# Down products of a mixture of experts in high and low parts: three fp32r products in place of one f32 product

## The reference

```python
shared = silu(flat @ sg) * (flat @ su) @ sd
probs = softmax(flat @ router_w)
topk_p, topk_i = top_k(probs, 2)
...
h = silu(einsum('nd,edf->nef', flat, wg)) * einsum('nd,edf->nef', flat, wu)
eo = einsum('nef,efd->ned', h, wd)
routed = einsum('ned,ne->nd', eo, cw)
return shared + routed
```

## Time and profile before

| What | Value |
|---|---|
| Median of 3 runs | 1467.71 us (1465.85 to 1470.97) |
| Profiled execution, own time | 1471.52 us |
| Its span | 1469.8 us (1.7 us of the time lie around it) |
| TensorE busy | 1393.9 us, 95% of the span |
| VectorE, ScalarE, GpSimd busy | 854.6, 795.2, 844.4 us |
| Mean granted clock of TensorE | 0.98 |
| The 15 expert blocks, first gate product to last down product | 1303 to 1462 us |

### The profile page before, as it was taken

How to read it: one execution, slowest core, us unless ns; L and a number is a source line. 1 busy time by engine, 2 the same in 40 slices (tenths; PEclk the granted TensorE clock), 3 DMA queues, 4 the chain that set the end, 5 groups by cost and what they waited for, 6 DMA issues and landing times. The chain is left out here.

```text
span 1469.8 us, 25247 instructions
## 1 busy us (share of the span) xinstructions
PE 1393.9 (95%) x8758; PEld 1138.3 (77%) x8758; DVE 854.6 (58%) x1433; ACT 795.2 (54%) x1229; POOL 844.4 (57%) x727
## 2 busy tenths in 40 slices
PE   4899999999999999999999999999998869999998
PEld 2578888888788888878888888888886447766664
DVE  7355655566456566655656566555553266657554
ACT  1346656665556665656666666666554222346552
POOL 3457767776667776767777777677665234110002
PEclk9999999999999999999999999999999979899999
DMA  5666676666666676656676676766756390369894
GB/s 208 207 107 126 115 135 108 125 117 133 114 121 122 112 129 114 133 107 123 117 136 123 108 137 119 134 108 112 147 94 136 109 335 0 129 217 371 332 374 151
DMA packets 115221, 218.46 MB, mean 149 GB/s; under 512 B 13312, under 2 KB 49152, under 8 KB 108928
## 3 DMA queue, kind: packets, MB, share of 16 engines
q1 hardware_dynamic: 111920, 209.00, 63.3%
q0 software_dynamic: 1280, 4.20, 0.9%
q10 hardware_dynamic: 1872, 3.41, 0.6%
HBM read 132.67 MB, written 16.78 MB: 102 GB/s over the span
## 5 line engine op out<-in xcount | busy, mean ns | idle before, releaser
L577 POOL TENSOR_TENSOR p_parts<-probs,p_parts 128x512 fp32r<-128x512 f32 x256 | 340.2, 1348 | 252.2 <-ACT p_parts L626 252.1
L626 ACT ACTIVATE p_parts<-probs 128x512 fp32r<-128x512 f32 x256 | 147.7, 624 | 247.6 <-PE banks L860 238.9
L728 DVE TENSOR_TENSOR probs<-banks,probs 128x1024 f32<-128x1024 f32 x128 | 156.7, 1224 | 161.6 <-ACT probs L632 161.6
L812 PE MATMUL banks<-wv_hi,x_hi 128*128 128x512 f32 x512 | 208.5, 407 | 4.8 <-PEq L170 4.8
L671 ACT ACTIVATE probs<-probs 128x1024 f32<-128x1024 f32 x128 | 135.9, 1062 | 142.2 <-POOL probs L584 141.9
L813 PE MATMUL banks<-wv_lo,x_hi 128*128 128x512 f32 x512 | 203.0, 396 | 0.0
L827 PE MATMUL banks<-x_hi,wk_hi 128*128 128x512 f32 x512 | 201.9, 394 | 0.0
L814 PE MATMUL banks<-wv_hi,x_lo 128*128 128x512 f32 x512 | 201.8, 394 | 0.0
L829 PE MATMUL banks<-x_hi,wk_lo 128*128 128x512 f32 x512 | 199.6, 390 | 0.0
L828 PE MATMUL banks<-x_lo,wk_hi 128*128 128x512 f32 x512 | 199.4, 389 | 0.0
L860 PE MATMUL banks<-p_parts,v_hi 128*65 128x128 f32 x1024 | 192.2, 224 | 0.0
(11 more groups left out here) (271 smaller groups left out, 2710.2 us busy)
## 6 DMA issues: line engine op xcount, KB each, us to landing
queries<-q_scratch SPq DMA_DIRECT2D x256, 128.0 KB, 6.0
keys<-wo_room SPq DMA_DIRECT2D x128, 256.0 KB, 5.6
keys<-turned_odd SPq DMA_DIRECT2D x128, 256.0 KB, 5.6
row_room<-in_ctx SPq DMA_DIRECT2D x64, 256.0 KB, 6.2
wo_room<-in_down SPq DMA_DIRECT2D x10, 1024.0 KB, 7.0
wo<-in_gate SPq DMA_DIRECT2D x8, 1024.0 KB, 8.3
gate_raw<-in_up SPq DMA_DIRECT2D x8, 1024.0 KB, 10.2
up_raw<-in_gate SPq DMA_DIRECT2D x7, 1024.0 KB, 9.1
```

What stands on the lines that cost most here:

```text
L577: nc.gpsimd.tensor_tensor(p_parts[:, 1, j, :], probs[:, pair % 2, j, :], p_parts[:, 0, j, :].bitcast(F32), ALU.subtract).then_inc(p_lo_rea ...
L728: nc.vector.tensor_tensor(mine, ps_s[:, :, :, 0, :].rearrange("p j i n -> p (j i) n"), mine, ALU.add).then_inc(s_taken, 1)
L812: nc.tensor.matmul(out, x_hi[:, buf, k, cols], wv_hi[:, k, heads], start=(k == 0), stop=False)
```

## The change

The down product of the expert blocks becomes `product` of high and low parts, like the gate and up products. The down weights are split by ScalarE (`down_high`, one copy of the whole 128x2048) and GpSimd (four subtractions, one for each tile t). Both parts have one room, that of `h_hi` and `h_lo`; `down_high(m)` therefore waits for the down product of block m-1. The turned hidden is split as well: `ht_hi` on ScalarE in the place of `ht`, `ht_lo` on VectorE (`hidden_low`) behind `hidden` of the next block. For the last block VectorE makes the low part of the weights in one operation. The gathers now go to two of the rooms of raw weights, and stand behind the 14 blocks' subtractions in GpSimd's program. `y` takes the place of `x3`. `load_down` waits for the low parts of the block three before. TensorE waits for `ht_lo_ready` and, tile by tile, for `down_lo_ready`.

```diff
-        y = sb("y", [P, BATCH, DIM])
+        y = x3
...
-        ht = sb("ht", [P, 2, KT, P])
+        ht_hi, ht_lo = (sb(n, [P, 2, KT, P], F32R) for n in ("ht_hi", "ht_lo"))
+
+        down_hi, down_lo = h_hi, h_lo
...
-        gathered = [h_hi.bitcast(F32), h_lo.bitcast(F32)]
+        gathered = [raw[1], raw[2]]
...
                 if j >= 3:
-                    sp.wait_ge(e_down_done, j - 2)
+                    sp.wait_ge(down_lo_ready, KT * (j - 2))
...
+            def gather():
+
+                pool.wait_ge(split_lo, unit_of(BLOCKS - LATE, UP) + 1)
+                for i in range(2):
+                    pool.wait_ge(e_stored[i], 16 * ((BLOCKS - LATE + 1 - i) // 2))
...
+            for m in range(BLOCKS - 1):
+                pool.wait_ge(down_hi_ready, m + 1)
+                for t in range(KT):
+                    nc.gpsimd.tensor_tensor(down_lo[:, t, :], down[m % 3][:, t, :], down_hi[:, t, :].bitcast(F32),
+                                            ALU.subtract).then_inc(down_lo_ready, 1)
+            gather()
...
+            def down_high(m):
+                act.wait_ge(down_landed[m % 3], 16 * (m // 3 + 1))
+                if m >= 1:
+                    act.wait_ge(e_down_done, m)
+                else:
+                    act.wait_ge(shared_done, BATCH)
+                nc.scalar.activation(down_hi, down[m % 3], ACT.Copy).then_inc(down_hi_ready, 1)
...
                 if j >= 1:
+                    down_high(j - 1)
                     act.wait_ge(h_turned, j)
                     if j >= 3:
                         act.wait_ge(e_down_done, j - 2)
-                    nc.scalar.activation(ht[:, (j - 1) % 2], ps_turn, ACT.Copy).then_inc(ht_ready, 1)
+                    nc.scalar.activation(ht_hi[:, (j - 1) % 2], ps_turn, ACT.Copy).then_inc(ht_hi_ready, 1)
...
+            def hidden_low(m):
+                dve.wait_ge(ht_hi_ready, m + 1)
+                nc.vector.tensor_tensor(ht_lo[:, m % 2], ps_turn, ht_hi[:, m % 2].bitcast(F32), ALU.subtract).then_inc(ht_lo_ready, 1)
...
                 nc.vector.tensor_tensor(hidden[:, j % 2, :], ps_up[:, 0, :], silu[:, j % 2, :], ALU.mult).then_inc(e_hidden_ready, 1)
+                if j >= 1:
+                    hidden_low(j - 1)
                 if j + 1 < BLOCKS:
...
+            dve.wait_ge(down_hi_ready, BLOCKS)
+            nc.vector.tensor_tensor(down_lo, down[(BLOCKS - 1) % 3], down_hi.bitcast(F32), ALU.subtract).then_inc(down_lo_ready, KT)
+            hidden_low(BLOCKS - 1)
...
                     if j >= 2:
-                        pe.wait_ge(ht_ready, j - 1)
+                        pe.wait_ge(ht_lo_ready, j - 1)
...
-                    pe.wait_ge(ht_ready, m + 1)
-                    pe.wait_ge(down_landed[m % 3], 16 * (m // 3 + 1))
+                    pe.wait_ge(ht_lo_ready, m + 1)
...
                     for t in range(KT):
-                        mm = nc.tensor.matmul(ps_y[:, m % 2, :], ht[:, m % 2, t, :], down[m % 3][:, t, :],
-                                              start=(t == 0), stop=(t == KT - 1))
+                        pe.wait_ge(down_lo_ready, KT * m + t + 1)
+                        mm = product(ps_y[:, m % 2, :], (ht_hi[:, m % 2, t, :], ht_lo[:, m % 2, t, :]),
+                                     (down_hi[:, t, :], down_lo[:, t, :]), t == 0, t == KT - 1)
                     mm.then_inc(e_down_done, 1)
```

More of the change, by code:

```diff
@@ L1363, in experts @@
         h_turned = sem("h_turned")
-        ht_ready = sem("ht_ready")
+        ht_hi_ready = sem("ht_hi_ready")
+        ht_lo_ready = sem("ht_lo_ready")
+        down_hi_ready = sem("down_hi_ready")
+        down_lo_ready = sem("down_lo_ready")
         e_down_done = sem("e_down_done")
@@ L1370, in experts @@
         out_ready = sem("out_ready")
-        first_added = sem("first_added")
+        shares_added = sem("shares_added")
         y_stored = sem("y_stored")
@@ L1376, in experts @@
         late_done = sem("late_done")
-        gathers_added = sem("gathers_added")
         def unit_of(j, w):
@@ L1430, in _ @@
         def _(pool):
+            def gather():
+                pool.wait_ge(split_lo, unit_of(BLOCKS - LATE, UP) + 1)
+                for i in range(2):
+                    pool.wait_ge(e_stored[i], 16 * ((BLOCKS - LATE + 1 - i) // 2))
+                for b in range(BATCH):
+                    for k in range(2):
+                        nc.gpsimd.indirect_dma_start(gathered[k][:, b, :], None, d["y_scratch"],
+                                                     bass.IndirectOffsetOnAxis(pos[:, k, b:b + 1], 0)).then_inc(fetched[b], 16)
             pool.wait_ge(keep["rows_zeroed"], 32)
@@ L1644, in _ @@
                 nc.vector.scalar_tensor_tensor(y[:, b, :], gathered[0][:, b, :], top[:, b, 0:1], y[:, b, :],
-                                               ALU.mult, ALU.add).then_inc(first_added, 1)
-                dve.wait_ge(first_added, b + 1)
+                                               ALU.mult, ALU.add).then_inc(shares_added, 1)
+                dve.wait_ge(shares_added, 2 * b + 1)
                 nc.vector.scalar_tensor_tensor(y[:, b, :], gathered[1][:, b, :], top[:, b, 1:2], y[:, b, :],
-                                               ALU.mult, ALU.add).then_inc(gathers_added, 1)
+                                               ALU.mult, ALU.add).then_inc(shares_added, 1)
             for b in range(BATCH):
-                dve.wait_ge(gathers_added, b + 1)
+                dve.wait_ge(shares_added, 2 * b + 2)
                 dve.wait_ge(late_done, b + 1)
```

## The result

The changed kernel takes 1503.97 us (median of 4 runs, 1498.3 to 1505.08); the kernel before 1466.78 us (4 runs, 1464.86 to 1470.97). The ratio is 1.024, with a 95% interval of 1.0205 to 1.0275: slower by 37 us. The profiled executions have spans of 1502.0 and 1469.8 us, 32.2 us apart; that of before was the slowest of its runs, so the spans show a little less than the medians.

What follows compares the result with a forecast made beforehand. TensorE, busy 95% of the span, was taken as the bound, with transfers filling 0.96 of queue time. Terms 2.8 + 32.35 + 0.9 + 1.8 = +37.9 us, on 1467.71 us, gave 1505.6 us; range 1480 to 1516.

Steps and rivals of the forecast that it cites:

- Block 0: First expert block: down_high behind the gate split and GpSimd slowed under VectorE's splits, +2.8 us (0.3 to 3.4).
- Twelve periods: The twelve block periods after block 0: 13.0 us each, 156 us against 123.65 now, +32.35 us.
- Iteration 14: No next splits and GpSimd undisturbed: 10.35 us against 9.41, +0.9 us.
- Tail: After the blocks: gathers queue behind GpSimd's low parts, start 8.1 us into iteration 14 and end last, +1.8 us.
- the main claim: Expert blocks: with one room, down_high waits for the previous down product, and making the weights' parts begins only there.
- The 1.5 us of hidden_low: Down product of each block: TensorE waits 1.5 us for hidden_low, which stands behind hidden on VectorE.
- GpSimd gives way, 1.8 us in each block: GpSimd's last subtraction: VectorE's split_low of up delays it 1.8 us (0 to 2.3), making the period 13.0 us.
- rival 2: Full lock: GpSimd loses VectorE's whole 2.29 us; period 13.5 us, +44.5 us, or 1512 us; chance 0.17.
- Rival 1: GpSimd is not slowed beside VectorE: period 10.9 to 11.2 us, +12.9 us, or 1481 us; chance 0.20.
- late_shares at 0: Iteration 3: late_shares, 5 us of VectorE, falls into waits that are there anyway and costs 0.
- The clock: Rival: new TensorE waits bring the clock to 1.2 GHz in each block; period 19.5 us, about 1580 us; chance 0.04.
- The stops on transfers: Expert blocks: TensorE's 3.2 us of stops for a next block's rows disappear inside the longer periods.

Runs made afterwards that it cites:

- vector_waits: Changed kernel, with VectorE's split_low of the next up weights waiting until GpSimd's four subtractions of the block are done; 1494.38 us, ratio 1.0181.
- two_rooms: Changed kernel with a second room for the down parts, so down_high and GpSimd's subtractions run a period earlier; 1487.17 us, ratio 1.0122.
- low_first: Changed kernel with VectorE making hidden_low ahead of hidden instead of behind it; 1509.26 us, ratio 1.0277.
- gpsimd_waits: Changed kernel, with GpSimd's last subtraction of each block waiting until VectorE's split_low of the next up weights is done; 1518.84 us, ratio 1.0358.
- spread: Changed kernel with late_shares cut into four parts, in iterations 1 to 4, each ahead of split_low of up; 1494.49 us, ratio 1.0188.
- two_low_spread: Changed kernel with a second room for the down parts, hidden_low ahead of hidden, and late_shares in four parts ahead of split_low of up; 1458.18 us, ratio 0.9948.

## Why the prediction was right, and where it was not

The total was met: +37.9 us forecast, +37.2 by the medians. Part of this is luck. The sum was made against the profiled span, and the spans are only 32.2 us apart, because the profiled execution before was the slowest of its kernel's. Here are its terms against the changed profile.

| Term | Forecast | Measured in the profiles |
|---|---|---|
| Stages ahead of the blocks (to the first rows_high) | 0 | -1.5 (1301.77, now 1300.23) |
| Block 0, to the first y copy | +2.8 | +1.1 |
| Twelve periods | +32.35 | +28.2 (151.83 - 123.65) |
| Iteration 14 | +0.9 | +1.1 |
| Tail | +1.8 | +3.4 |
| Span | +37.9 | +32.2 |

**The places in the block were right to a few hundredths.** By the y copy at 1397.85: down_high 2.88 (forecast 2.88), GpSimd's first tile 4.86 (4.88), hidden 6.35 and hidden_low 6.96 (both as forecast), TensorE's first down matmul 7.70 (7.70). The base period of 11.2 us is 11.22 to 11.24, and vector_waits has it in eleven blocks. Two_rooms shows the main claim, that one room makes the chain the bound. Block 0 came out 1.7 us under its term, because GpSimd was not made to give way there: its four took 5.72 us.

**The 1.5 us of hidden_low was rightly placed in the chain's shadow.** The sum took its wait and the GpSimd chain as one path, not as two costs; low_first bears that out.

**The term "GpSimd gives way, 1.8 us in each block" was wrong in its mechanism.** Its size is that of no block: the cost is 2.1 us or nothing. The Trainium skill's rule (SBUF — State Buffer, Who interferes with whom: an exclusive lock for the whole instruction), which I had weighed against the earlier trace rows and set aside, holds here in both directions. My misreading was of a merged row: GpSimd's 2.97 and 3.02 us are pairs, and VectorE's operation came 1.06 and 1.20 us in, just ahead of the border between the two tiles at about 1.27. That fits an entry at the border and not in the middle: GpSimd's second tile ends 1.14 us behind VectorE's operation in both pairs, and in the long block its fourth ends 1.12 us behind VectorE's split_low (1402.71 + 7.39 against 1406.69 + 2.29). With the full price my rival 2 gives 13.5 us a period, and gpsimd_waits takes 13.55; the naturally long blocks take 13.3. Rival 1's 11.2 are the short blocks. The truth is a mixture of my rivals 1 and 2: seven short and four long among the twelve periods, and the one with late_shares.

**late_shares at 0 was wrong.** By my own places its 5 us end 8.83 + 2.29 + 5 = 16.1 us after a y copy, so 3.1 us into the next iteration, where VectorE's next split is due at 3.0. But it ended 7.7 us in (1354.10 against the y copy at 1346.41). Of the 4.6 us between, 2.0 are the two operations that waited for GpSimd, 1.1 the split in front that came late at the low clock, 1.1 the block itself (11.86 us and not 13.0), and 0.3 its own length. The iteration took 17.75 us against 11.22 or 13.30.

**The twelve periods came out near the forecast by luck.** Against 13.0 us each, seven short blocks saved 12.5 us; the iteration of late_shares gave back 4.8, low clock 2.3, and the four long blocks 1.2. That leaves 4 us less than forecast. Who goes first at the port decides the first of these and a part of the second.

**The clock.** I had the clock fall in every block or in none. In this profile it fell in three of the twelve besides the iteration of late_shares: at the end of the first long block and behind it (13.82 and 11.86 us, granted 0.96 and 0.91), and behind a later long block (12.35 us, 0.86). Against 13.30 and 11.22 us that is 2.3 us together. The Trainium skill (TensorE: Matmul & The Clock Gate, Part 1) has the array gated when idle. The stop of 2.26 us in the block at 1397.85 left the clock at 1.00, one of 2.25 us before 1434.68 did not.

**The tail** was 1.6 us longer than forecast. The gathers began 8.19 us after iteration 14's start (8.1 forecast), but from the first issue to the last gather's first use it took 14.6 us (13.07 forecast). One of the issues took 2.81 us, others 0.95 to 1.16 (the row at 1485.82). VectorE's low part of the last block's weights had started 0.3 us before it and ended at 1487.81, 0.82 us before the issue did. The changed kernel and all nine versions of it have this meeting, at different moments of the issue: it takes 1.89 to 2.81 us and always ends 0.81 to 0.83 us behind VectorE's operation of 2.3 us. So here GpSimd's issue waits for VectorE as well. Beside VectorE's shorter operations of 0.75 us it takes 0.95 to 1.48 us. The rows:

```profile
1485.52 2.29 DVE L1672 TENSOR_TENSOR wk_hi<-wo_room,wk_hi 128x2048 fp32r<-128x2048 f32 x1 [5.65 <-ACT wk_hi L1485]
...
1495.36 0.75 DVE L1677 SCALAR_TENSOR_TENSOR x<-up_raw,top,x 128x512 f32<-128x512 f32 x1 [1.34 <-DMA down_raw<-y_scratch,pos]
...
1498.01 1.28 DVE L1685 TENSOR_TENSOR x<-ps_gate,x 128x512 f32<-128x512 f32 x2
```

**The stops on transfers** did disappear, as I said.

What stays open: why VectorE's and GpSimd's requests fall 0.05 us earlier or later from block to block, and what decides whether a stop brings the clock down. Neither was tried.

## What to carry to other kernels

A split of operands into high and low parts paid here only once the parts were made a whole period ahead. With one room for them, the product that they make faster stands at the end of a chain that begins when it ends, and that turned 0.63 us of gain a block into 1.4 to 3.5 us of loss; a second room and one reordering gave it back. A wait in the shadow of another costs nothing until the other is gone, so a reordering that gained nothing alone should be tried again after the bound has moved. Where two engines hold each other up, find out which order is the cheap one and set it by a wait rather than leave it to chance: with GpSimd first the blocks took 11.2 us, with VectorE first 13.5, and nearly the same in every block either way. And a total that was met says little until its terms are compared: here errors of 12 and 8 us in opposite directions met.

## What the runs showed of the hardware that I had not expected

VectorE's two-input operation and GpSimd's subtractions take turns in full, at the borders of instructions, and who goes first is a race of a few hundredths of a microsecond. Over four of the runs (the changed kernel, low_first, spread, two_rooms) I took the start of VectorE's split_low of up less the start of GpSimd's four. At 3.99 us or less VectorE won every time, 12 of 12, and GpSimd took 7.37 to 7.44 us. From 4.04 to 5.1 us GpSimd won every time, with 5.32 to 5.73 us, and VectorE took up to 3.4. From 4.01 to 4.03 us it went either way. In one kernel this makes periods of 11.2 and 13.3 us with nothing else changed, and it is a part of the spread between runs (1498.3 to 1505.08 us) that was not taken apart.

GpSimd's issue of an indirect transfer was held up too, in ten kernels by an operation of VectorE with two inputs in SBUF: it ended 0.81 to 0.83 us behind it each time (the tail, above).

The transfers reached 411 GB/s and a share of 1.02 over a block in two_low_spread without holding TensorE up, where the kernel before had two of its three stops on the rows in iterations of 333 and 372 GB/s. Its blocks take 9.20 us, those of the kernel before at least 9.83, so the rate alone does not explain the stops. The moment at which the loads are issued may; no run changed that alone.
